# Two-layer transformer kernel: the phase after the delta rule reordered (row sums and masked values earlier, two bank pairs for the gated FFN, two squares on VectorE, a first group of its own)

## The reference, cut to what matters

```python
y = y * rsqrt(mean(y * y, -1) + EPS) * head_norm_w            # y: output of the delta rule, 8 heads of 64
gate = sigmoid(silu(x @ Wu1 + bu1) @ Wu2 + bu2)
y = x + y @ Wo * gate
z = _rms(y, ff_norm_w)
y = y + silu(z @ Wff1) * (z @ Wff3) @ Wff2                    # 128 -> 512 -> 128
x = x0 + ga * y
h = _layernorm(x) * (1 + cb) + sb
x = x + gb * (gelu(h @ w1 + b1) @ w2 + b2)
# layer 1
h = _layernorm(x) * (1 + ca1) + sa1
attn = softmax(where(band, q @ k2.T / sqrt(8), neg))          # per window and head, 32 x 64
x = x + ga1 * ((attn @ v2) @ wo.T)
h = _layernorm(x) * (1 + cb1) + sb1                           # then a second layer norm with gamma, beta
x = x + gb1 * (h + 0.5 * (silu(ln(h) @ w1q + fc1_bias) @ w2q + fc2_bias))
```

## Time and profile before

| what | value |
| --- | --- |
| median of 3 runs | 1542.05 us (1540.95 to 1544.72) |
| profiled execution: its own time | 1541.44 us |
| its span | 1539.7 us |
| busy: PE, DVE, ACT, POOL | 74%, 67%, 41%, 4% of the span |
| TensorE clock granted, mean | 0.85 of full |
| post phase | from about 1049 us to the end, some 490 us |

### The profile page before, as it was taken

The page is one execution under the profiler, slowest core; times in us unless marked ns, Lnnn a source line. Parts: engine busy times, 40 slices in busy tenths (PEclk is TensorE's granted clock), DMA queues, the critical chain, the costliest instruction groups (busy, mean ns, idle before and its releaser), DMA issues. The chain is left out here.

```text
span 1539.7 us, 23379 instructions
## 1 busy us (share of the span) xinstructions
PE 1146.2 (74%) x7956; PEld 836.2 (54%) x7956; DVE 1026.5 (67%) x3365; ACT 629.5 (41%) x868; POOL 63.8 (4%) x78
## 2 busy tenths in 40 slices
PE   2097776059888888998888888875668788787885
PEld 1042332038787777887777788773226335354372
DVE  4779999888878788788887887851324243362261
ACT  2257665224333333343433344323254363462522
POOL 2000000100000000000000000001111011020000
PEclk9588887569999999899999999996786887988956
DMA  2002332301100100110011000002000000000000
GB/s 80 0 1 109 137 132 84 120 14 36 34 33 14 34 34 20 34 34 17 31 34 34 20 34 34 18 4 64 0 1 1 0 7 1 0 8 0 0 8 7
DMA packets 27211, 49.09 MB, mean 32 GB/s; under 512 B 4246, under 2 KB 8919, under 8 KB 27162
## 3 DMA queue, kind: packets, MB, share of 16 engines
q1 hardware_dynamic: 25642, 47.02, 8.9%
q10 hardware_dynamic: 1520, 1.48, 0.4%
HBM read 26.47 MB, written 22.02 MB: 31 GB/s over the span
## 5 line engine op out<-in xcount | busy, mean ns | idle before, releaser
L920 PE MATMUL ps<-delta_tm,drive 128*128 128x128 f32 x768 | 106.7, 296 | 3.8 <-DVE delta_zb L1046 3.8
L920 PEld LDWEIGHTS ps<-delta_tm,drive 128*128 128x128 f32 x768 | 98.2, 205 | 9.4 <-DVE delta_zb L1046 5.9
L931 PE MATMUL ps<-delta_tt,delta_xf 128*128 128x64 f32 x768 | 101.5, 275 | 0.0
L929 PE MATMUL ps<-delta_xf,delta_tt 128*128 128x64 f32 x768 | 99.8, 274 | 0.0
L929 PEld LDWEIGHTS ps<-delta_xf,delta_tt 128*128 128x128 f32 x768 | 94.6, 194 | 0.0
L931 PEld LDWEIGHTS ps<-delta_tt,delta_xf 128*128 128x128 f32 x768 | 93.5, 192 | 0.0
L779 ACT ACTIVATE delta_xf<-ps 128x256 f32<-128x256 f32 (+1 forms) x128 | 48.9, 382 | 106.0 <-PE ps L920 86.1
L1203 DVE TENSOR_TENSOR delta_tm<-delta_tm,ps 128x256 f32<-128x256 f32 x96 | 40.3, 419 | 76.6 <-PE ps L931 75.6
L892 PEld LDWEIGHTS ps<-delta_kq_up,delta_arena 64*128 64x128 f32 x1024 | 74.1, 225 | 22.3 <-DVE delta_diag L1161 15.1
L892 PE MATMUL ps<-delta_kq_up,delta_arena 64*128 64x128 f32 x1024 | 80.3, 318 | 1.4
L551 DVE SCALAR_TENSOR_TENSOR kept<-mem 128x32 f32<-128x32 f32 x384 | 73.3, 191 | 1.6 <-PEq L79 1.0
(11 more groups left out here) (365 smaller groups left out, 2673.4 us busy)
## 6 DMA issues: line engine op xcount, KB each, us to landing
kq_store<-prep_unit SPq DMA_DIRECT2D x8, 1024.0 KB, 4.2
zb_store<-prep_zb_cols SPq DMA_DIRECT2D x8, 1024.0 KB, 5.7
delta_zb<-zb_store SPq DMA_DIRECT2D x16, 512.0 KB, 3.5
delta_kq<-kq_store SPq DMA_DIRECT2D x16, 512.0 KB, 3.2
v_store<-prep_v_rows SPq DMA_DIRECT2D x4, 1024.0 KB, 6.6
delta_v<-v_store SPq DMA_DIRECT2D x16, 256.0 KB, 2.6
out<-post_rows SPq DMA_DIRECT2D x4, 256.0 KB, 2.3
setup_wmod<-in_L_wmod ACTq DMA_DIRECT2D x2, 384.0 KB, 4.2
```

Source lines behind the costliest of these rows:

```text
L920: ins = eng.matmul(m.ps[:, 4 + n, P * (h % 4):P * (h % 4) + P], bt[s][:, h, :], m.tm[:, h, :], start=True, stop=True)
L929: eng.matmul(m.ps[:, 6 + n, HD * (h % 4):HD * (h % 4) + HD], m.tt[:, h, :], cols(m.xf[:, h, :], 0), start=True, stop=True)
L931: ins = eng.matmul(m.ps[:, 6 + n, 256 + HD * (h % 4):256 + HD * (h % 4) + HD], m.xf[:, h, :], cols(m.tt[:, h, :], 1), start=True, stop=True)
```

## The change

It reorders calls inside the passes, gives the gated FFN a second pair of banks (2 and 3, free once `pt3` has been copied out), lets DVE compute two squares that ACT computed, splits `gelu_hidden` and `last_hidden` so that a mean of the other part fits between, and gives the first group its own order: `gate_in` waits for the two loads that it reads, `scales` and the dequantization come later, and the four products of `normed(0)` go from POOL to DVE.

```diff
 @@ SP
-            for dst, src in mixer_loads:
+            for dst, src in mixer_loads[:2]:
+                eng.dma_start(dst, src).then_inc(gate_w_in, 16)
+            for dst, src in mixer_loads[2:]:
                 eng.dma_start(dst, src).then_inc(mixer_in, 16)
 @@ POOL
-            for i in range(NGRP):
+            queries(0)
+            for i in range(1, NGRP):
                 normed(i)
                 queries(i)
 @@ ACT, silu_gate and the loop
-                eng.activation(m.hid_e[:, f % 2, :], m.ps[:, 6, :], ACT.Silu)...
+                eng.activation(m.hid_e[:, f % 2, :], m.ps[:, 6 - 4 * (f % 2), :], ACT.Silu)...
                 if mix:
-                    z_root(j)
+                    z_square(j)
                 if win:
                     weights_out(i, 3)
                 if mix:
+                    mix_root("z", j, 1)
...
                 if win:
                     win_square("n3", i)
-                    win_bias(i)
...
                 if win:
-                    win_square("n4", i)
                     win_root("n4", i)
+                    win_bias(i)
                     silu_out(i)
...
                 if mix:
-                    mix_square("n2", j)
                     mix_root("n2", j, 0)
 @@ PE, the steps
             def gate_in(i):
...
-                    eng.wait_ge(mixer_in, 16 * len(mixer_loads))
+                    eng.wait_ge(gate_w_in, 32)
             def project(i):
...
-                eng.wait_ge(mix_pool, mpool.at("yn3", i))
+                if i:
+                    eng.wait_ge(normed_done, npool.at("yn3", i - 1))
+                else:
+                    eng.wait_ge(first_normed, NP)
             def gated_hidden(i, f):
-                if f:
-                    eng.wait_ge(mix_scalar, mact.at(f"a{f - 1}_e", i))
+                b = 6 - 4 * (f % 2)
+                if f > 1:
+                    eng.wait_ge(mix_scalar, mact.at(f"a{f - 2}_e", i))
+                elif f == 0:
+                    eng.wait_ge(mix_vector, mvec.at("z", i))
+                elif i:
+                    eng.wait_ge(win_scalar, wact.at("pt3", i - 1))
                 else:
-                    eng.wait_ge(mix_vector, mvec.at("z", i))
-                eng.matmul(m.ps[:, 6, :], m.wff1[:, P * f:P * f + P], m.xc_a[:, :], start=True, stop=True)
-                if f:
-                    eng.wait_ge(mix_vector, mvec.at(f"a{f - 1}", i))
-                eng.matmul(m.ps[:, 7, :], m.wff3[:, P * f:P * f + P], m.xc_a[:, :], ...)
+                    eng.wait_ge(pre_vector_done, pre_vec.at("fc1_b"))
+                eng.matmul(m.ps[:, b, :], m.wff1[:, P * f:P * f + P], m.xc_a[:, :], start=True, stop=True)
+                if f > 1:
+                    eng.wait_ge(mix_vector, mvec.at(f"a{f - 2}", i))
+                eng.matmul(m.ps[:, b + 1, :], m.wff3[:, P * f:P * f + P], m.xc_a[:, :], ...)
             def mix_var(p, i):      # and win_var for n4 in the same way
-                eng.wait_ge(mix_scalar, mact.at(f"{p}_sq", i))
+                if p == "n1":
+                    eng.wait_ge(mix_scalar, mact.at("n1_sq", i))
+                else:
+                    eng.wait_ge(mix_vector, mvec.at("n2_sq", i))
 @@ PE, the loop
                 if mix:
                     gate_in(j)
-                if i == -1:
-                    scales()
...
                 if mix:
                     y_sums(j, 1)
+                if i == -1:
+                    gate(j)
+                    scales()
...
                     own(i, 2)
                     values(i, 3)
                 if mix:
-                    for f in range(NF):
+                    gated_hidden(j, 0)
+                if win:
+                    own(i, 3)
+                if mix:
+                    for f in range(1, NF):
                         gated_hidden(j, f)
-                if win:
-                    own(i, 3)
-                if mix:
                     gated_out(j)
...
                 if mix:
-                    gelu_hidden(j)
+                    gelu_hidden(j, range(3))
                 if win:
                     win_mean("n4", i)
+                if mix:
+                    gelu_hidden(j, range(3, NF))
+                if win:
                     win_var("n4", i)
                 if mix:
                     gelu_out(j)
                 if win:
-                    last_hidden(i)
+                    last_hidden(i, range(2))
                 if mix:
                     mix_mean("n2", j)
+                if win:
+                    last_hidden(i, range(2, NF))
+                if mix:
                     mix_var("n2", j)
 @@ DVE
-                eng.wait_ge(mixer_in, 16 * len(mixer_loads))
+
+            def output_weights():
+
+                eng.wait_ge(mixer_in, 16 * len(mixer_loads) - 32)
                 for c in range(NP):
                     ins_ = eng.tensor_scalar(m.wo[:, c, :], m.wo[:, c, :], m.head_norm[:, c:c + 1], None, ALU.mult)
+            def first_group(c):
+
+                eng.wait_ge(mix_scalar, mact.at(f"y_r{c // 2}", 0))
+                r = m.y_sq[:, GT * c:GT * c + GT].rearrange("p (n t) -> p n t", n=GROUP)
+                eng.tensor_tensor(m.yn[:, GT * c:GT * c + GT].rearrange("p (n t) -> p n t", n=GROUP), y_of(0)[:, c], r, ALU.mult)...
+            def mix_square(i):      # and win_square(i) for n4 in the same way
+                eng.wait_ge(mix_vector, mvec.at("n2_cen", i))
+                eng.tensor_tensor(m.sq_a[:, :], m.xc_a[:, :], m.xc_a[:, :], ALU.mult)...
 @@ DVE, the loop
                     gate_mid(j)
                 if i == -1:
-                    residual_gates()
+                    output_weights()
+                    for c in range(NP):
+                        first_group(c)
...
                     gate_floor(j)
                 if i == -1:
-                    quantized()
+                    residual_gates()
                 if win:
                     own(i, 0)
                     row_sums(i, 1)
                     weights(i, 3)
                     own(i, 1)
+                    row_sums(i, 2)
                 if mix:
                     gated(j)
+                if i == -1:
+                    quantized()
+                if win:
+                    own(i, 2)
+                    row_sums(i, 3)
+                if mix:
                     z_norm(j)
                 if i == -1:
                     last_biases()
                 if win:
-                    row_sums(i, 2)
-                    own(i, 2)
+                    own(i, 3)
                 if mix:
                     for f in range(NF):
                         gated_hidden(j, f)
                 if win:
-                    row_sums(i, 3)
-                    own(i, 3)
                     history(i)
```

More of the change, by code:

```diff
@@ L1460, in post_phase @@
         mix_vector = ctx.enter_context(nc.semaphore("mixer_vector_done"))
-        mvec = steps("g0 gu s0 gated y1 z " + each("a{0}", 4) + " y2 x1 n1_cen n1_nrm x2 n2_cen n2_nrm")
+        mvec = steps("g0 gu s0 gated y1 z " + each("a{0}", 4) + " y2 x1 n1_cen n1_nrm x2 n2_cen n2_sq n2_nrm")
         mix_scalar = ctx.enter_context(nc.semaphore("mixer_scalar_done"))
         mact = steps("y_sq0 y_sq1 g_e g_ln g_sig y_ln0 y_ln1 y_ln2 y_ln3 y_r0 y_r1 s_e s_ln s_sig z_sq z_ln z_r " + each("a{0}_e", 4)
-                     + " n1_sq xb n1_ln n1_r " + each("gelu{0}", 4) + " n2_sq n2_ln n2_r hc qc kc v2a v2b")
+                     + " n1_sq xb n1_ln n1_r " + each("gelu{0}", 4) + " n2_ln n2_r hc qc kc v2a v2b")
         mix_tensor = ctx.enter_context(nc.semaphore("mixer_tensor_done"))
@@ L1467, in post_phase @@
         mix_pool = ctx.enter_context(nc.semaphore("mixer_pool_done"))
-        mpool = steps(each("yn{0}", NP) + " " + each("qm{0}", GROUP))
+        mpool = steps(each("qm{0}", GROUP))
+        normed_done = ctx.enter_context(nc.semaphore("mixer_normed_by_pool"))
+        npool = steps(each("yn{0}", NP))
+        first_normed = ctx.enter_context(nc.semaphore("first_group_normed"))
         win_vector = ctx.enter_context(nc.semaphore("windows_vector_done"))
@@ L1473, in post_phase @@
                      + " ".join(f"sum{n} rec{n} rm{n} own{n}" for n in range(2, GROUP))
-                     + " hist x3 n3_cen n3_nrm h3 n4_cen n4_nrm zh x4")
+                     + " hist x3 n3_cen n3_nrm h3 n4_cen n4_sq n4_nrm zh x4")
         win_scalar = ctx.enter_context(nc.semaphore("windows_scalar_done"))
-        wact = steps("exp0 pt0 exp1 pt1 exp2 pt2 exp3 pt3 ao n3_sq xb n3_ln n3_r n4_sq n4_ln n4_r " + each("b{0}_e", 4) + " rows")
+        wact = steps("exp0 pt0 exp1 pt1 exp2 pt2 exp3 pt3 ao n3_sq n3_ln n3_r n4_ln n4_r xb " + each("b{0}_e", 4) + " rows")
         win_tensor = ctx.enter_context(nc.semaphore("windows_tensor_done"))
@@ L1528, in normed @@
                     r = m.y_sq[:, GT * c:GT * c + GT].rearrange("p (n t) -> p n t", n=GROUP)
```

(32 more changed lines are left out.)

15 lines of the change are left out of this document (12 added, 3 removed).

## The result

The changed kernel takes 1460.4 us (median of 4 runs, 1458.6 to 1471.4) against 1543.4 (4 runs): a ratio of 0.948, 95% interval 0.9435 to 0.952. Run again beside the last experiments it took 1460.5 (5 runs, 1456.9 to 1462.0), ratio 0.945 (0.9436 to 0.9462). The forecast was 1468 within 1455 to 1486. The profiled execution took 1458.59 us, 82.9 under the one of before.

A forecast was written before the change was run, and what follows sets the result against it. PE was taken as the engine to look at, its waits paid twice, as hole and low clock behind. Mixed passes 58.2 plus first pass 15.2 make 73.4 us off 1541.44: 1468, range 1455 to 1486.

The forecast's parts named there:

- the first pass: Pass ahead of the loop: earlier gate, head products on DVE and earlier projection save 15.2 us, between 11 and 20.
- the clock's charge: Mixed passes: 2 us a pass deducted because narrow products `own2` and `pv3` might bring the low clock.
- pass 3: Last pass: DVE order the same, PE never ahead of it; gain 0, by -1 to +3 for the clock.
- Up to `ff2`, pass 1: Mixed pass 1 up to `ff2`: no wait of `own2`, full clock behind it and a faster FFN save 17.0 us.
- the hole of 4.7: PE's wait ahead of `own2` in pass 1, for DVE's masked values: it goes, 4.7 us.
- From `n1` to q: Mixed pass, `n1` to q: earlier means and DVE squares bring q 3.1 us earlier, between 1.5 and 3.8.
- the rival: Clock falls between `zs` and `a0`: 5.4 of 20.1 us lost per mixed pass, whole 1478; chance 0.22.
- Pass 0 ahead of `zs`: Stretch of pass 0 before the end of `zs`, where the prediction's sums for mixed passes start: no gain counted.
- all goes well: No low clock from `zs` to each pass's end, first pass at full clock saving 20: 1457 us; chance 0.13.
- The rule on cycling through PSUM banks: Short idle times between matmul groups make the clock swing; by it the FFN's two pairs could lose what they gain.
- The rival at 1492: FFN clock swings at the new pairs, 6.9 us more a mixed pass; 1486 to 1505 has chance 0.10.
- The slower rival: Mixed passes held at the low clock throughout by narrow products following one another: 1667 us; chance 0.02.

The follow-up runs named there:

- Undoing the order alone: Changed kernel with DVE's row sums and masked values of rounds 2 and 3 back behind z and the FFN products, own3 behind a3: 1498.4 us.
- fillers: Matmul products without a reader; two added to the changed kernel in the wait ahead of the third scores, passes 0 to 2: 1455.0 us.
- the last of them: Changed kernel with the first group's four head products on GpSimd again instead of VectorE: 1472.9 us.

## Why the prediction was right, point by point

The measured 1460.4 lies in the stated range, 7.6 us under the 1468 of the forecast. By the profiles the change gave 82.9 us for the predicted 73.4. The mechanism is the predicted one; of the difference, 5.8 us come from a stretch to which the prediction gave nothing, 2.8 from the first pass, 1.5 from the clock's charge, and -0.7 from pass 3.

- **Up to `ff2`, pass 1:** predicted 17.0 us, measured 16.9 (32.7 to 15.8). Each of its terms is in the rows: the hole of 4.7 gone, `own2` and `pv3` 2.9 us, `a0` at 1.12 for its first two instructions, 1.41 ahead of `ff2`. Undoing the order alone brings 8.6 us of holes and 12.6 us a pass back.
- **From `n1` to q:** predicted 3.1 us, measured 2.8: before, 1326.25 (start of `n1`'s mean) to 1354.84; after, 1264.44 to 1290.22. `w2` starts 1.6 us earlier from the same point (predicted 2.0). The sum was right for both edits together, but they are not 3.1 shared out: undone one by one they cost 5 and 9 us a pass without fillers.
- **The clock's charge** was 2 us a pass. From the end of `zs` on the three passes gave 21.1, 19.7 and 18.9 us, against 23.1, 20.1 and 21.0 without the charge: 2.0, 0.4 and 2.1 less. So in passes 0 and 2 the clock did fall between `zs` and `a0`, as the rival had it, but later than in the rival: `own2` and `pv3` ran at the upper level (0.97 and 1.97 us), and only `a0` did not. Its first two instructions in passes 0 and 2, which took 1.12 us in pass 1:

```profile
1165.21 2.04 PE L1793 MATMUL ps<-post_xc_a,post_wff 128*128 128x512 f32 x2
1332.48 2.06 PE L1793 MATMUL ps<-post_xc_a,post_wff 128*128 128x512 f32 x2
```

In the second profile of the changed kernel this happens in pass 1 alone. The charge had the right size for two passes of three, on another product than the one it was made for.
- **Pass 0 ahead of `zs`** was the term put at nothing, and it gave the most of what the forecast lacked, 5.8 us. The same stretch, before and after:

```profile
1148.10:1186.40 38.30, 34.73 (x262) 24.58 (x261) 22.39 (x28) 18.83 (x22) 5.94 (x4) 0.73 0.00 1
1130.10:1162.60 32.50, 28.58 (x266) 20.59 (x265) 26.84 (x34) 19.68 (x23) 6.13 (x4) 0.89 0.00 1
```

For PE it is the same work at a higher granted clock: its busy time falls by 6.2 us. In passes 1 and 2 this stretch took 34.1 us before and 34.2 and 34.0 after. The prediction's sums start at the end of `zs` and let it be; why the clock was low for so long there before is open.
- **Which case came:** 1460.4 lies under 1462, in the case "all goes well" (0.13). But that case's conditions, no low stretch from `zs` on and 20 us from the first pass, were not met. The time fits it through the 5.8 us in pass 0 that no case had. That is luck.
- **First pass:** predicted 15.2 us, measured 18.0. The projection started at 1070.05 (predicted 1070.7): 14.3 us for 13.6. It ran in 5.19 us instead of 6.74: 1.5 us that I had put only in the upper end. From there to `a0` 5.8 us for 6.0, where I had charged half a microsecond; the FFN 11.3 us (predicted 11.1). The four strided head products took 3.84 us (I took 4). In the second profile of the changed kernel the projection took 6.61 us, so that the 1.5 us are not sure to come. I put the wait of 7.55 us ahead of the old projection down to VectorE, as the row names it; the code waits there for GpSimd's last head product, which ended at 1084.21, 0.15 us before the projection started.
- **Pass 3:** predicted 0, measured -0.7, inside its bounds.
- **The rule on cycling through PSUM banks** of the Trainium skill (TensorE: Matmul & The Clock Gate, section "A second HAM failure mode: psum-queue depth-cycling"): the trace does not show it here. In the two-pair FFN of pass 1 PE is busy for 8.09 of 9.50 us and the granted clock is 1.00:

```profile
1249.70:1259.20 9.50, 8.09 (x27) 3.88 (x25) 3.60 (x8) 3.30 (x6) 0.00 (x0) 1.00 0.00 0
```

In passes 0 and 2 `a0` is low, and `a1` to `a3` are at the upper level (1.02 to 1.10 us for two instructions). The rival at 1492 falls.
- **The slower rival** (mixed passes held at the lower level by narrow products) did not come as such. But its mechanism is real: pass 3 was held there and lost 12.5 us to it, and stretches of 20 us and more at the lower level cost some 6 to 8 us a pass (5.9 with the scale products first, 6.2 and 7.8 between the passes of the kernel with ScalarE's squares). I had given it a place in all passes at once or none. My argument against it, that every row of wide products brings the clock back, does not hold: within the 20 us at 0.55 and 0.50 shown above there are four wide instructions in 2.85 us and two more in 1.91.

What stays open: why the same hole is followed by 3 us at 1.2 GHz in one run and by 20 in another. The two profiles differ in what was done passes earlier (the scale products in pass -1), but runs of one kernel differ among themselves too, and no run here says by what.

## What to carry to other kernels

Price a wait on the matmul engine twice, as the hole and as the narrow work behind it at half clock, and look for the hole's successor in the list of waits: on that reading 17.0 us were forecast for pass 1 up to `ff2` and 16.9 measured. Ask also for stretches at the lower level outside the part that the change touches: one of them gave 5.8 us that no term had. The price of an edit that opens a hole is not fixed: undone one by one, the edits that together gave 83 us cost 38, 24, 28, 16, 23 and 12 us by the medians, and the last of them nothing in two of its six runs. To compare variants more cleanly, fill the waits with wide products that nobody reads first: the spread of the runs fell from 7.1 to 1.2 us and from 18.4 to 3.6; where a stretch of narrow products runs at the lower level, such products can pay for themselves.

## What the hardware showed unexpectedly

- 22 products of 128x512 without a reader made a pass 12.5 us shorter, at a granted clock of 0.93 in place of 0.59. In the kernel before, PE was busy without a break on narrow products in the window of the earlier trace rows and got 0.50.
- VectorE's small steps stretch while GpSimd runs: three of five steps on 128x4 took 1.37 to 1.43 us beside GpSimd's products, the two others 0.16, and all five take 0.16 to 0.19 in the changed kernel, where GpSimd does nothing beside them. GpSimd's four products take 5.93 us, so one ends about every 1.5 us (an estimate), and each stretched step ends within 0.1 us of such an end. From the trace with the head products on GpSimd:

```profile
1061.28 5.93 POOL L1535 TENSOR_TENSOR drive<-mem,drive 128x512 f32<-128x512 f32 x4 [8.09 <-ACT drive L1582]
1061.43 1.39 DVE L2047 TENSOR_TENSOR post_gate_s<-post_gate_s,mod_cols 128x4 f32<-128x4 f32 x1
```

and from that of the changed kernel:

```profile
1066.57 0.17 DVE L2051 TENSOR_TENSOR post_gate_s<-post_gate_s,mod_cols 128x4 f32<-128x4 f32 x1
```
